# Attention scores and value products with the high and low halves side by side in 320 columns, and eight steps moved

## The reference

```
xn  = layernorm(x)
h   = relu(xn @ nm_w1 + nm_b1);   m = h @ nm_w2 + nm_b2
q, k, v = m @ q_w + q_b, m @ k_w + k_b, m @ v_w + v_b
att = softmax over the keys within 32 positions of (q . k) / sqrt(128), times v
score   = sigmoid(xn @ gate_w.T)                  # 16 experts
combine = the 8 experts with the largest score + bias, scores normalised, times 2.826
ffn = sum over 16 experts of combine * down(silu(gate(xn)) * up(xn))  +  one shared expert
out = x + att + ffn
```

## Time and profile before

| | |
|---|---|
| median of three runs | 686.98 us |
| the profiled execution, whole | 687.21 us |
| its span in the trace | 685.4 us |
| PE busy | 676.9 us, 99% |
| PEld busy | 553.8 us, 81% |
| DVE busy | 597.6 us, 87% |
| ACT busy | 437.2 us, 64% |
| POOL busy | 443.0 us, 65% |
| PE clock granted | 0.999 of full |

### The profile page before, as it was taken

One profiled execution on the slowest core, in us unless ns is written; L12 is line 12 of the kernel. 1 busy time (PEld: TensorE's weight loads), 2 busy tenths in 40 slices (PEclk: granted clock), 3 DMA queues, 4 the chain that ended last, 5 costly groups with the idle time before them and its releaser, 6 DMA issues.

```text
span 685.4 us, 10455 instructions
## 1 busy us (share of the span) xinstructions
PE 676.9 (99%) x3172; PEld 553.8 (81%) x3172; DVE 597.6 (87%) x1640; ACT 437.2 (64%) x874; POOL 443.0 (65%) x400
## 2 busy tenths in 40 slices
PE   7999999999999999999999999999999999999997
PEld 6877788888888888888888888888888888888885
DVE  7998989888889898889888898898889888898775
ACT  5775656657675575666657665575756757666573
POOL 4785666666667756766666667766667567666553
PEclk9999999999999999999999999999999999999999
DMA  8607255252623617155261633617145161631500
GB/s 266 236 9 272 61 186 185 93 232 73 233 113 124 235 46 277 62 173 198 65 260 51 252 116 104 254 45 278 63 163 208 49 262 47 220 121 63 231 0 16
DMA packets 38040, 101.80 MB, mean 149 GB/s; under 512 B 8672, under 2 KB 18144, under 8 KB 29920
## 3 DMA queue, kind: packets, MB, share of 16 engines
q1 hardware_dynamic: 37984, 101.14, 41.1%
HBM read 92.42 MB, written 8.70 MB: 148 GB/s over the span
## 4 chain that ended last, share of the span: by engine, by line
PE 90%; DVE 4%; DMA 3%; ACT 1%; issue 1%; SPq 1%; POOL 0%; DVEq 0%; ACTq 0%
PE ps_y L486 26%; PE ps_u L476 26%; PE ps_g L466 25%; PE bank L408 3%; PE bank L447 3%; PE bank L430 3%; PE bank L437 1%; PE ps_y L456 1%; DMA exp_raw<-wexp 1%; DMA h_dram<-exp_raw 1%; DVE ps_u L1134 1%; PE bank L419 1%; DVE h_lo L1140 1%; DMA exp_raw<-h_dram 0%; DVE prob_n L1037 0%
## 5 line engine op out<-in xcount | busy, mean ns | idle before, releaser
L1262 POOL TENSOR_TENSOR silu_c<-silu,comb_b 128x512 f32<-128x512 f32 x252 | 325.3, 1294 | 220.5 <-ACT silu L717 219.6
L725 ACT ACTIVATE h_hi<-ps_u 128x512 fp32r<-128x512 f32 x272 | 162.9, 599 | 232.9 <-DVE ps_u L1134 232.8
L1140 DVE TENSOR_TENSOR h_lo<-ps_u,h_hi 128x512 fp32r<-128x512 f32 x272 | 186.0, 684 | 37.3 <-ACT h_hi L725 30.4
L1134 DVE TENSOR_TENSOR ps_u<-silu_c,ps_u 128x512 f32<-128x512 f32 x256 | 177.1, 692 | 28.5 <-PE ps_u L476 24.2
L717 ACT ACTIVATE silu<-ps_g 128x512 f32<-128x512 f32 x272 | 162.0, 596 | 0.2
L476 PE MATMUL ps_u<-xn_hi,exp_w_hi 128*128 128x512 f32 x272 | 111.2, 409 | 0.7 <-DVE h_lo L1140 0.6
L486 PE MATMUL ps_y<-h_hi,exp_w_hi 128*128 128x512 f32 x272 | 109.4, 402 | 0.9 <-DVE h_lo L1140 0.4
L466 PE MATMUL ps_g<-xn_hi,exp_w_hi 128*128 128x512 f32 x272 | 108.1, 397 | 1.3 <-ACT silu L717 1.3
L486 PE MATMUL ps_y<-h_lo,exp_w_hi 128*128 128x512 f32 x272 | 107.7, 396 | 0.0
L476 PE MATMUL ps_u<-xn_hi,exp_w_lo 128*128 128x512 f32 x272 | 107.6, 396 | 0.0
L486 PE MATMUL ps_y<-h_hi,exp_w_lo 128*128 128x512 f32 x272 | 107.3, 394 | 0.0
(11 more groups left out here) (156 smaller groups left out, 989.2 us busy)
## 6 DMA issues: line engine op xcount, KB each, us to landing
comb_b<-c_dram SPq DMA_DIRECT2D x63, 1024.0 KB, 7.2
mom_b<-st_dram SPq DMA_DIRECT2D x13, 512.0 KB, 3.7
xres<-x_t SPq DMA_DIRECT2D x16, 256.0 KB, 2.6
out_t<-xres SPq DMA_DIRECT2D x16, 256.0 KB, 2.0
xin<-x SPq DMA_DIRECT2D x15, 256.0 KB, 3.2
h_dram<-exp_raw SPq DMA_DIRECT2D x60, 64.0 KB
exp_raw<-h_dram SPq DMA_DIRECT2D x15, 256.0 KB, 3.1
xn<-x_t SPq DMA_DIRECT2D x13, 256.0 KB, 3.3
```

What stands on the lines that cost most here:

```text
L725: A(h_t[hbuf(par, s)][0][:], ps_u[(par + s) % 2][:], ACT.Copy).then_inc(s_h_hi, 1)
L1134: V.tensor_tensor(ps_u[i][:], src[:], ps_u[i][:], ALU.mult).then_inc(s_h, 1)
L1140: V.tensor_tensor(t[1][:], ps_u[(par + s) % 2][:], t[0][:].bitcast(F32), ALU.subtract)\
L1262: G.tensor_tensor(silu_c[i][:], silu[i][:], comb_b[:, s1 - 1, :], ALU.mult).then_inc(s_silu_c, 1)
```

## The change

In groups 2 to 15 (`wide(g)`), the scores take the high and low half of the keys in one matmul of 320 columns, whose two halves land side by side in PSUM, and a second matmul of 160 columns adds low query by high key to the first half. The high and low keys lie in one tensor for that. ACT copies the second half with the key term added to SBUF (`low_scores`), POOL adds the mask to it, and DVE's row_max adds the sum to the first half; row_max, the exponentials and normalise_probs now keep their values in SBUF (`prob`). In all groups, `attend` does the same with the probabilities: per key block one matmul of 320 and one of 160 columns, each sequence in its own bank. z_hi is then two instructions of 256 columns, and z_lo four, in two rounds with a wait between.

Pieces move: scores of sequence 0 from slot 3 to 2; POOL's second mask_terms from 3 to 5; exponentials from slots 5 and 6 to 6 and 7; row_max of sequence 1 and normalise_probs of sequence 0 from 6 to 7; turn_probs and prob_hi from 7 and 9 to 8 and 10; prob_lo of sequence 1 from 10 to 11; route_scores from between h_prod and h_lo to behind h_lo in slot 7; moments from 15 to 13; variance from slot 0 to slot 15 of the group before; q_lo from before h_lo to behind it in slot 16. At the very end value_proj comes behind the first of the last three down products.

The diff, cut to its core:

```diff
+        def wide(g):
+            return g + 1 >= TURNED
...
-            def scores(seq):
+            def scores(g, seq):
+                if wide(g):
+                    for t in range(2):
...
+                        dst = window_bank[t]
+                        mm(dst[:, 0:2 * WIN].rearrange("p (h c) -> p h c", h=2), q_t[0][:, q0:q0 + P],
+                           hid_hl[:, :, k], start=True, stop=False, skip_group_check=True)
+                        done = mm(dst[:, 0:WIN], q_t[1][:, q0:q0 + P], hid_hl[:, 0, k], start=False, stop=True,
+                                  skip_group_check=True)
...
             def attend(seq):
+                dst = att_bank[seq]
                 for kb in range(2):
-                    col = seq * SEQ + kb * (P - HALF)
-                    for n, (a, b) in enumerate(PAIRS3):
-                        wide = SEQ if kb == 0 and n == 0 else WIN
-                        done = mm(bank[2][:, col:col + wide], hid_n[a][:, seq * 2 + kb, :],
-                                  p_t[b][:, seq, kb, 0:wide], start=kb == 0 and n == 0, stop=kb == 1 and n == 2,
-                                  skip_group_check=True)
+                    c = slice(kb * (P - HALF), kb * (P - HALF) + WIN)
+                    mm(halves(dst)[:, :, c], hid_n[0][:, seq * 2 + kb, :], p_t[:, :, seq, kb, :],
+                       start=kb == 0, stop=False, skip_group_check=True)
+                    done = mm(dst[:, c], hid_n[1][:, seq * 2 + kb, :], p_t[:, 0, seq, kb, :],
+                              start=False, stop=kb == 1, skip_group_check=True)
...
-                if s == when(g, 3, 5):
+                if s == when(g, 2 if wide(g) else 3, 5):
...
                 if s == when(g, 5, 7):
-                    scores(1)
+                    if wide(g):
+                        pe.wait_ge(S["nmax0"], g + 1)
+                    scores(g, 1)
...
-                if s == when(g, 7, 10):
+                if s == when(g, 7, 10) and not last(g):
+                    hid_proj(g + 1, 1 - par)
+                if s == when(g, 8, 10):
                     pe.wait_ge(S["pn0"], g + 1)
...
                     turn_probs(0)
-                    if not last(g):
-                        hid_proj(g + 1, 1 - par)
...
+            def low_scores(g, seq):
+                act.wait_ge(S[f"sc{seq}"], g + 1)
+                act.wait_ge(S["key_term"], 2 * g + seq + 1)
+                for t in range(2):
+                    n = 2 * seq + t
+                    done = A(low_k[:, n, :], window_bank[t][:, WIN:2 * WIN], ACT.Identity, bias=key_term[:, n:n + 1])
+                done.then_inc(S[f"low{seq}"], 1)
...
+                if wide(g) and s == 2:
+                    low_scores(g, 0)
+                if wide(g) and s == 5:
+                    low_scores(g, 1)
-                if s == when(g, 5, 8):
+                if s == when(g, 6, 8):
                     if more:
                         gate_exp(g + 1)
                     prob_exp(g, 0)
...
-                if s == when(g, 6, 9):
+                if s == when(g, 7, 9):
                     prob_exp(g, 1)
...
             def z_lo(g):
                 dve.wait_ge(S["z_hi"], g + 1)
-                V.tensor_tensor(z_t[1][:], bank[2][:], z_t[0][:].bitcast(F32), ALU.subtract).then_inc(S["z_lo"], 1)
+                for seq in range(NB):
+                    c = slice(seq * SEQ, (seq + 1) * SEQ)
+                    done = V.tensor_tensor(z_t[1][:, c], att_bank[seq][:, 0:SEQ], z_t[0][:, c].bitcast(F32),
+                                           ALU.subtract)
+                done.then_inc(S["z_rest"], 1)
+                dve.wait_ge(S["z_rest"], g + 1)
+                for seq in range(NB):
+                    c = slice(seq * SEQ, (seq + 1) * SEQ)
+                    done = V.tensor_tensor(z_t[1][:, c], att_bank[seq][:, SEQ:2 * SEQ], z_t[1][:, c].bitcast(F32),
+                                           ALU.add)
+                done.then_inc(S["z_lo"], 1)
...
-                if s == when(g, 6, 9):
+                if s == when(g, 7, 9):
                     normalise_probs(g, 0)
-                if s == 7 and more and not first(g):
-                    route_scores(g + 1)
...
-                if s == 0 and TURNED < g + 2 < GROUPS:
-                    variance(g + 2)
...
+                if s == 13 and TURNED < g + 3 < GROUPS:
+                    moments(g + 3, 1 - par)
                 if s == 15 and TURNED < g + 3 < GROUPS:
-                    moments(g + 3, 1 - par)
+                    variance(g + 3)
...
+                if s == STEPS - 1 and not last(g):
+                    q_lo(g + 1)
+                if s == when(g, 7, 9) and not last(g):
+                    route_scores(g + 1)
```

More of the change, by code:

```diff
@@ L118, in layer @@
         hid = sb("hid", [P, T])
-        hid_t = [sb("hid_hi", [P, T], F32R), sb("hid_lo", [P, T], F32R)]
+        hid_hl = sb("hid_hl", [P, 2, T], F32R)
+        hid_t = [hid_hl[:, half, :] for half in range(2)]
         q_t = [sb("q_hi", [P, T], F32R), sb("q_lo", [P, T], F32R)]
@@ L221, in layer @@
             hid_mm hid hid_hi hid_lo q_mm q_hi q_lo hid_tp hn_hi hn_lo key_term
-            mask_k sc0 sc1 nmax0 nmax1 exp0 exp1 inv0 inv1 pn0 pn1 pt0 pt1
-            p0_hi p0_lo p1_hi p1_lo pv z_hi z_lo""".split()
+            low0 low1 mask_k sc0 sc1 nmax0 nmax1 exp0 exp1 inv0 inv1 pn0 pn1 pt0 pt1
+            p0_hi p0_lo p1_hi p1_lo pv z_hi z_rest z_lo""".split()
         S = {n: sem(n) for n in names}
@@ L596, in att_early @@
                     pe.wait_ge(S["q_lo"], g + 1)
-                    scores(0)
+                    if g + 1 == TURNED:
+                        pe.wait_ge(S["xn_lo"], TURNED)
+                    scores(g, 0)
                 if s == when(g, 4, 7) and more:
@@ L623, in att_late @@
                     pe.wait_ge(S["p1_lo"], g + 1)
+                    pe.wait_ge(S["hid_hi"], g + 1 + (not last(g)))
                     attend(1).then_inc(S["pv"], 1)
@@ L698, in z_hi @@
                 act.wait_ge(S["pv"], g + 1)
-                A(z_t[0][:], bank[2][:], ACT.Copy).then_inc(S["z_hi"], 1)
+                for seq in range(NB):
+                    done = A(z_t[0][:, seq * SEQ:(seq + 1) * SEQ], att_bank[seq][:, 0:SEQ], ACT.Copy)
+                done.then_inc(S["z_hi"], 1)
+            def low_scores(g, seq):
[5 more added lines that the diff above has]
+                done.then_inc(S[f"low{seq}"], 1)
             def prob_exp(g, seq):
@@ L704, in prob_exp @@
                     n = 2 * seq + t
-                    win = score_bank[seq][:, t * SEQ:t * SEQ + WIN]
-                    done = A(win, win, ACT.Exp, scale=-1.0,
+                    done = A(scored(g, seq, t), scored(g, seq, t), ACT.Exp, scale=-1.0,
                              bias=neg_max[:, n:n + 1], accum_out=row_sum[:, n:n + 1])
@@ L711, in prob_hi @@
                 act.wait_ge(S[f"pt{seq}"], g + 1)
-                A(p_t[0][:, seq, :, 0:WIN], windows(score_bank[seq]), ACT.Copy).then_inc(S[f"p{seq}_hi"], 1)
+                A(p_t[:, 0, seq, :, :], windows(score_bank[seq]), ACT.Copy).then_inc(S[f"p{seq}_hi"], 1)
             def gate_silu(g, par, s):
@@ L1023, in row_max @@
                     n = 2 * seq + t
-                    win = score_bank[seq][:, t * SEQ:t * SEQ + WIN]
+                    src = window_bank[t][:, 0:WIN] if wide(g) else score_bank[seq][:, t * SEQ:t * SEQ + WIN]
                     done = V.tensor_tensor_reduce(
-                        out=win, in0=win, in1=mask_k[:, n, :],
+                        out=scored(g, seq, t), in0=src, in1=mask_k[:, n, :],
                         scale=-1.0, scalar=-TAKEN, op0=ALU.add, op1=ALU.min, accum_out=neg_max[:, n:n + 1])
@@ L1102, in att @@
                     z_lo(g)
-                    if more:
-                        q_lo(g + 1)
             def fresh_att(s):
@@ L1157, in slot @@
                     moments(1, 1)
-                if first(g) and s == 9:
-                    route_scores(1)
+                if s == STEPS - 1 and not last(g):
+                    q_lo(g + 1)
+                if s == when(g, 7, 9) and not last(g):
+                    route_scores(g + 1)
             def finish():
@@ L1241, in mask_terms @@
             def mask_terms(g, seq):
+                if wide(g):
+                    n = slice(2 * seq, 2 * seq + 2)
+                    pool.wait_ge(S[f"low{seq}"], g + 1 - (TURNED - 1))
+                    G.tensor_tensor(mask_k[:, n, :], mask[:], low_k[:, n, :], ALU.add).then_inc(S["mask_k"], 1)
+                    return
                 pool.wait_ge(S["key_term"], 2 * g + seq + 1)
@@ L1276, in slot @@
                     mask_terms(g, 0)
-                if s == when(g, 3, 6):
+                if s == when(g, 5 if wide(g) else 3, 6):
                     mask_terms(g, 1)
```

38 lines of the change are left out of this document (27 added, 11 removed).

## The result

| | before | changed |
|---|---|---|
| median of the runs | 687.00 us | 719.58 us (719.30 to 719.67, 4 runs) |
| ratio | | 1.0473, 95% interval 1.0455 to 1.0491 |
| span of the profiled execution | 685.4 us | 717.8 us |
| a group | 41.35 us | 43.63 us |
| PE busy | 99% | 95% |

The change makes the kernel slower by 4.7%, 33 us, more than five times the 5.8 us of the forecast and outside its range. The sign and the wait that it named came; a larger one came beside it.

What follows compares the result with a forecast made beforehand. PE, busy 99%, was taken to set the pace. A full group: -0.84 saved, +0.85 silu wait, +0.2 and +0.2 lateness = +0.41 us; with first and last groups +5.8 on 687.21, so 692.8 us; range 685 to 700.

Steps and rivals of the forecast that it cites:

- the wait that it named: PE waits for the silu of step 8 at the gate product of step 10, 0.6 to 0.9 us each.
- What bounds the kernel: PE, busy 99%, sets the pace; tightest place the silu of step 7, with 0.35 us of slack.
- PE's saving: Scores and attend blocks on PE: 0.47 us in place of 0.68, saving 0.21 a block, bounds nothing and 0.24.
- the sign of being right: In the new trace, a block of scores on PE would span 0.43 to 0.48 us.
- The estimate by the Trainium skill: By the page's spacings a PE block goes from 0.51 to 0.38 us and saves 0.13.
- The late silu: Silu of step 8 ends at T + 10.37; PE waits 0.74 at the gate product of step 10, 0.85 with restart.
- T: Start of h_prod of step 4 on DVE, 362.26 us in the trace of the kernel before.
- z_lo: On DVE, four instructions of 256 columns in two rounds: 1.46 us against 0.60, 0.86 more.
- T itself: DVE comes late to h_prod of step 4: 0.2 us a group, bounds 0 and 0.5.
- The second stall at step 12: Up product of step 12: PE waits for h_lo of step 10, 0.2 us a group, bounds 0 and 0.45.
- The rival of no gain or a gain: Delays cancel the saving, within 1.4 us of 687.0, 18%; or PE keeps its saving, mostly near 683, 22%.
- Its best case: Gate product of step 10: no other delays, block saving 0.24, exp in SBUF free; gain 0.24 a group, 684.5 us.

Runs made afterwards that it cites:

- the whole change placed anew: Changed kernel with q_lo in slot 1, second key_terms in slot 2 and hid_n_lo on POOL in slot 6: 693.02 us, ratio 1.0092.
- the placement with slot 6: Kernel before with new attend and z_lo, q_lo, key_terms, moments and variance moved, hid_n_lo on POOL in slot 6: 685.06 us, ratio 0.9972.
- with slot 10: Kernel before with new attend and z_lo and the same pieces moved, but hid_n_lo on POOL in slot 10: 682.65 us, ratio 0.9933.
- The control: Same placement on the kernel before, attend and z_lo as they were; run with hid_n_lo on POOL in slot 6 only: 689.56 us, ratio 1.0036.

## Why the prediction was wrong

- **What bounds the kernel**: right. PE at 99% and others with slack measured in tenths (the list of waits has one of 1.4 us at the start of the program that the text passes over); but I looked for the tightest place on ACT alone. xres was as tight. In the kernel before, the down product of step 0 starts at 358.09 and xres ends at 357.20 + 0.74 = 357.94, 0.15 us earlier; the block of scores stood between, and moving it to slot 2 took 0.68 us of cover away.
- **PE's saving**: 0.16 us a block in place of 0.21, inside its bounds, but outside the 0.43 to 0.48 us named as the sign of being right (0.52 measured). The first pair is as fast as estimated (0.14 and 0.08), the second 320 columns cost 0.18. The estimate by the Trainium skill, "TensorE: Matmul & The Clock Gate", section "Back-to-back issue gap", was a saving of 0.13; the measured 0.16 lies between it and mine, though the page's spacings themselves aren't those of the trace.
- **The late silu**: right. h_prod of step 4 starts at 377.77 and silu of step 8 ends at 387.44 + 0.60 = 388.04, T + 10.27 against T + 10.37; the wait is 0.71 + 0.11 against 0.74 + 0.11:

```profile
387.44 0.60 ACT L773 ACTIVATE silu<-ps_g 128x512 f32<-128x512 f32 x1
```

- **z_lo**: right in size, 363.64 - 362.18 = 1.46.
- **T itself**, the lateness of DVE at h_prod of step 4, is the step that failed. It was put at 0.2 us a group with 0.5 as its upper bound, "the latter if its SBUF operands meet POOL's". DVE's stretch took 16.20 us (377.77 - 361.57) where 14.43 were worked out. Three holds lie in it, 0.56 + 1.02 + 0.64 = 2.22 us against the instructions' free lengths. The missing 1.8 us don't need all of them: with xn_lo free T stayed where it was, and DVE waited 0.38 us for PE there. The first two make DVE late to h_lo and xres, and with them PE. I had priced a meeting at an instruction's own size; it costs what is left of POOL's instruction, whatever the size of DVE's, and there was more than one. And I had asked only whether z_lo itself meets POOL, not which instructions behind it do once they start later against silu_c.
- **The way to PE** was missing too. I looked at T, where DVE feeds the chain of the exponentials, and not at h_lo of step 0 and xres on the way there. They cost PE 0.67 + 1.12 + 0.22 = 2.01 us a group. This, and not the lateness at T, is what the group pays: the wait for the silu is counted from T.
- **The second stall at step 12**: right. h_lo of step 10 ends at 395.54 + 0.65 = 396.19, T + 18.42, against T + 18.5, and the up product of step 12 loses 0.05 + 0.11 = 0.16 us, against 0.2.
- **The rival of no gain or a gain** had no support in the whole change, though its half, attend, has it: 4.5 us, in a placement where none of the three is held. Its best case was put too well: it adds 0.05 for the restart where the sum has 0.11, so by its own terms it is a gain of 0.18 a group, about 685 us and not 684.5.

By measured terms a group is -0.64 + 0.82 + 2.01 + 0.16 - 0.08 = +2.27 against +2.28. How the two parts of the +2.01, cover moved away and holds, share it is known only within bounds: without the three holds 0.45 of it is left at xres, with the old attend 0.32 (hid_n_lo being still held by a quarter of a us), with the whole change placed anew 0.11. So 1.56 of it go with the holds. Of the 0.18 us a group that the placement with slot 6 costs, 0.15 are seen at the up product of step 10; with slot 10 that stall is gone. The control with slot 10 wasn't run, so what attend alone is worth there isn't shown.

## What to carry to other kernels

Before more work is given to DVE beside a busy POOL, list the DVE instructions behind it that read two tensors from SBUF, and where POOL's tensor-tensor instructions fall when all of that starts later. A form that shows two durations in one trace (0.68 and 1.07 us here) says that it happens already. And where PE's work is moved, look at what it covered: the wait that becomes visible is at the old place, not at the new one.
